# A Mamba-2 mixer with a 4-bit feed-forward layer: y and z laid out channel-major, the heads' products in two column tiles

## What is computed

```python
z, xBC, dt = split(u @ W_in)                 # z: 512 channels, x: 512, B: 128, C: 128, dt: 8
xBC = silu(causal_conv4(xBC) + conv_b)
x, B, C = split(xBC)
dt = softplus(dt + dt_bias);  A = -exp(A_log)
y = ssd(x * dt, A * dt, B, C)                # y_l = sum_{s<=l} (C_l.B_s) exp(sum_{s<r<=l} A dt_r) dt_s x_s
y = y + x * D                                # D: one number per head
y = y * silu(z)
y = y * rsqrt(mean(y**2) + eps) * norm_scale
x1 = layernorm(u + y @ W_out)
out = layernorm(x1 + ffn(x1))                # 256 -> 2048 -> 256, gate and up, 4-bit weights with scales
```

## Time and profile before

| | us |
|---|---|
| median of 3 runs | 983.26 (981.26 to 985.05) |
| profiled execution, its time | 982.58 |
| its span, first to last instruction | 980.8 |
| TensorE busy | 921.1 (94%) |
| VectorE busy | 682.8 (70%) |
| ScalarE busy | 535.3 (55%) |
| GpSimd busy | 85.0 (9%) |

### The profile page before, as it was taken

How to read it: one execution, slowest core, us unless ns; L and a number is a source line. 1 busy time by engine, 2 the same in 40 slices (tenths; PEclk the granted TensorE clock), 3 DMA queues, 4 the chain that set the end, 5 groups by cost and what they waited for, 6 DMA issues and landing times.

```text
span 980.8 us, 16203 instructions
## 1 busy us (share of the span) xinstructions
PE 921.1 (94%) x5452; PEld 798.0 (81%) x5452; DVE 682.8 (70%) x1390; ACT 535.3 (55%) x1056; POOL 85.0 (9%) x170
## 2 busy tenths in 40 slices
PE   4677889899999999999999999999999999999997
PEld 3446668788888888878888888878888889888887
DVE  6776667687758876687758766687759765776453
ACT  4643478357645576447645575447645674455232
POOL 2110000200002000200011000200011001100000
PEclk9797999899999999999999999999999999999999
DMA  4111000010001000020001000020001000000000
GB/s 132 31 57 48 25 23 22 1 55 1 20 3 66 0 0 21 0 65 0 22 0 65 0 0 21 1 65 0 22 0 65 1 2 12 22 33 1 1 33 11
DMA packets 18813, 23.28 MB, mean 24 GB/s; under 512 B 1728, under 2 KB 15296, under 8 KB 18752
## 3 DMA queue, kind: packets, MB, share of 16 engines
q1 hardware_dynamic: 18176, 22.56, 7.1%
q10 hardware_dynamic: 576, 0.03, 0.0%
HBM read 14.19 MB, written 4.19 MB: 19 GB/s over the span
## 4 chain that ended last, share of the span: by engine, by line
issue 54%; PE 31%; DVE 7%; POOL 4%; ACT 3%; DMA 1%; POOLq 0%; SPq 0%; DVEq 0%; ACTq 0%
PE up_bank L482 2%; PE mixer L562 2%; PE down L482 2%; PE down L483 2%; PE up_bank L484 2%; PE down L484 2%; PE up_bank L483 2%; PE gate_bank L482 2%; PE gate_bank L483 2%; PE gate_bank L484 2%; PE mixer L482 2%; PE mixer L484 2%; PE mixer L483 2%; DVE xbc L898 1%; PE down L642 1%
## 5 line engine op out<-in xcount | busy, mean ns | idle before, releaser
L482 PE MATMUL down<-wd_hi,in_hi 128*128 128x256 f32 x512 | 145.1, 283 | 0.6 <-DVE in_lo L1019 0.6
L483 PE MATMUL down<-wd_lo,in_hi 128*128 128x256 f32 x512 | 144.6, 282 | 0.0
L484 PE MATMUL down<-wd_hi,in_lo 128*128 128x256 f32 x512 | 144.3, 282 | 0.0
L898 DVE SCALAR_TENSOR_TENSOR xbc<-mixer,chan,xbc 128x510 f32<-128x510 f32 (+1 forms) x162 | 111.0, 685 | 32.9 <-ACT xbc L690 30.5
L768 ACT ACTIVATE act_sb<-gate_bank 128x512 f32<-128x512 f32 (+1 forms) x144 | 79.0, 549 | 86.1 <-PE gate_bank L484 84.9
L754 ACT ACTIVATE in_hi<-act_sb 128x512 fp32r<-128x512 f32 (+1 forms) x144 | 83.5, 580 | 68.9 <-PE down L484 55.5
L1033 DVE SCALAR_TENSOR_TENSOR act_sb<-up_bank,act_sb 128x512 f32<-128x512 f32 (+1 forms) x144 | 90.5, 628 | 40.1 <-PE up_bank L484 22.3
L482 PE MATMUL up_bank<-hT_hi,wu_hi 128*128 128x512 f32 (+1 forms) x288 | 108.2, 376 | 7.0 <-DVE act_sb L1033 6.8
L482 PE MATMUL gate_bank<-hT_hi,wg_hi 128*128 128x512 f32 (+1 forms) x288 | 114.2, 396 | 0.0
L484 PE MATMUL gate_bank<-hT_hi,wg_lo 128*128 128x512 f32 (+1 forms) x288 | 107.6, 374 | 0.0
L483 PE MATMUL gate_bank<-hT_lo,wg_hi 128*128 128x512 f32 (+1 forms) x288 | 107.1, 372 | 0.0
(11 more groups left out here) (201 smaller groups left out, 2031.7 us busy)
## 6 DMA issues: line engine op xcount, KB each, us to landing
xbc<-in_u_t_dram SPq DMA_DIRECT2D x7, 512.0 KB, 3.6
h_sb<-in_u_dram SPq DMA_DIRECT2D x7, 512.0 KB, 3.9
h_res<-h_sb SPq DMA_DIRECT2D x7, 512.0 KB, 2.9
out_dram<-h_res SPq DMA_DIRECT2D x7, 512.0 KB, 3.3
scales<-in_ffn_s_dram SPq DMA_DIRECT2D x24, 128.0 KB, 2.1
packed<-in_ffn_w_dram SPq DMA_DIRECT2D x8, 96.0 KB, 2.0
xbc<-in_u_t_dram SPq DMA_DIRECT2D x2, 256.0 KB, 2.8
xbc<-in_W_in_dram SPq DMA_DIRECT2D x1, 512.0 KB, 6.2
```

The lines of the kernel that those rows point to most:

```text
L482: nc.tensor.matmul(dst, lh, rh, start=first, stop=False, skip_group_check=True)
L483: nc.tensor.matmul(dst, lh, rl, start=False, stop=False, skip_group_check=True)
L484: return nc.tensor.matmul(dst, ll, rh, start=False, stop=last, skip_group_check=True)
L898: ins = stt(acc[:, :, d:], src[:, :, 0:SEQ - d], chan[:, c:c + 1], acc[:, :, d:], ALU.mult, ALU.add)
```

## The change

z is projected channel-major like x (4 blocks of 128 channels in every group, the halved groups too, which now have z2 and z3). In Y the operands change places: `xdt` (64 columns of a head) is stationary, the decay matrix of 128 columns is moved, and the even heads write partitions 0 to 63, the odd ones 64 to 127, each in a column tile of its own. y so comes out channel-major. D is now one number per partition, and x is used as it is, channel-major: VectorE's `x_d` adds it in four 128-column steps. The state's decay must now stand along the free axis, alike on all partitions of a head: a new product E, from the same R as D, in four 512-column matmuls per pair of tiles (two with 128 output rows, two with 64), and ScalarE's Exp of 512 columns of it in the item Y of odd tiles. The gated y needs no transpose: `gT` and its bank go. Its squares are added over blocks by VectorE and over partitions by a one-column matmul, S; VectorE scales that and GpSimd raises it to the power -1/2 in one step. CB loses its two 8-column matmuls. The load of the next transposed u waits for the last `x_d` instead of the last XT, since x is read longer. In the tables `gT` becomes `g`, and S is set into the slots:

```diff
 USES (full):
-             "D0a", "D0b", "Y0", "XT1", "D1a", "D1b", "Y1", "Yoff0", "CB1", "gT0", "XT2", "D2a", "D2b",
-             "op0", "gT1", "Y2", "XT3", "D3a", "D3b", "op1", "gT2", "Y3", "Yoff1", "op2", "gT3", "op3"],
+             "D0a", "D0b", "Y0", "XT1", "D1a", "D1b", "E0", "Y1", "Yoff0", "CB1", "XT2", "D2a", "D2b", "S0",
+             "op0", "Y2", "XT3", "D3a", "D3b", "E1", "S1", "op1", "Y3", "Yoff1", "S2", "op2", "S3", "op3"],
 SLOTS (full):
-             ["D0"], ["R1", "Y0", "XT1"], ["D1"], ["R2", "Y1", "CB1", "gT0", "XT2"], ["D2"],
-             ["R3", "op0", "gT1", "Y2", "XT3"], ["D3"], ["op1", "gT2", "Y3"], ["op2", "gT3"], ["op3", "ln1"], ["ln2"]],
+             ["D0"], ["R1", "Y0", "XT1"], ["D1"], ["R2", "Y1", "CB1", "g0", "XT2"], ["D2", "S0"],
+             ["R3", "op0", "g1", "Y2", "XT3"], ["D3", "S1"], ["op1", "g2", "Y3"], ["S2", "op2", "g3"],
+             ["S3", "op3", "ln1"], ["ln2"]],
...
+        D_ADDED, Y_DONE = (1, 4, 7, 10), (2, 6, 8, 12)
...
-                wait_for((ready(g - 1, f"XT{tiles(g - 1) - 1}")[0], g - 1, ready(g - 1, f"XT{tiles(g - 1) - 1}")[1]))
+                wait_for((y_step, g - 1, D_ADDED[tiles(g - 1) - 1]))
                 sp.dma_start(u32[:, :, 0:width(g)], uT_of(g)).then_inc(uT_in.sem, 16)
 TensorE:
-                    nc.tensor.matmul(b[:, 3 * P:3 * P + H], tri_r[:, :], dA_hi[:, 2 * i + 1, :],
-                                     start=True, stop=False)
-                    nc.tensor.matmul(b[:, 3 * P:3 * P + H], tri_r[:, :], dA_lo[:, 2 * i + 1, :],
-                                     start=False, stop=True).then_inc(ready(g, use)[0].sem, 1)
...
+                    if i % 2:
+                        use = f"E{i // 2}"
+                        wait_bank(pe, use, g)
+                        for a, rows in ((1, P), (0, HP)):
+                            for n, part in enumerate(R_of(g)):
+                                mm = nc.tensor.matmul(bank(g, use)[0:rows, :],
+                                                      tri_r[:, P - 1:P].to_broadcast([P, rows]), part[:, a::2, :],
+                                                      start=n == 0, stop=n == 1, skip_group_check=True)
...
                     for h in range(H):
-                        mm = nc.tensor.matmul(bank(g, use)[:, h * HP:(h + 1) * HP], dec_of(g, i)[:, h, :],
-                                              xdt[:, h * HP:(h + 1) * HP], start=True, stop=True)
+                        j, a = h // 2, h % 2
+                        mm = nc.tensor.matmul(bank(g, use)[a * HP:(a + 1) * HP, j * P:(j + 1) * P],
+                                              xdt[:, h * HP:(h + 1) * HP], dec_of(g, i)[:, h, :],
+                                              start=True, stop=True, tile_position=(0, a * HP), skip_group_check=True)
...
-                        nc.tensor.matmul(bank(g, use)[:, :], cb[:, 1, :], xtail[:, :], start=True,
-                                         stop=True).then_inc(ready(g, use)[0].sem, 1)
-                elif kind == "gT":
-                    use = f"gT{i}"
-                    wait_bank(pe, use, g)
-                    wait(pe, y_step, g, (3, 8, 11, 16)[i])
-                    for j in range(JT):
-                        mm = nc.tensor.transpose(bank(g, use)[:, j * P:(j + 1) * P],
-                                                 zs[:, i, j * P:(j + 1) * P], ident[:, :])
+                        for j in range(JT):
+                            mm = nc.tensor.matmul(bank(g, use)[:, j * P:(j + 1) * P], xtail[:, j * P:(j + 1) * P],
+                                                  cb[:, 1, :], start=True, stop=True)
+                elif kind == "S":
+                    wait_bank(pe, name, g)
+                    wait(pe, sq_sum, g, i + 1)
+                    nc.tensor.matmul(bank(g, name)[:, 0:1], y[:, i % 2, 0:P], tri[:, P - 1:P], start=True,
+                                     stop=True).then_inc(ready(g, name)[0].sem, 1)
 ScalarE:
-                        nc.scalar.activation(e2[:, i // 2, :], bank(g, f"CB{i // 2}")[:, 3 * P:3 * P + H],
-                                             ACT.Exp).then_inc(e2_ok.sem, 1)
...
+                elif kind == "Y":
+                    if i % 2:
+                        if i > 2:
+                            wait_ready(act, f"S{i - 2}", g)
+                        wait_ready(act, f"E{i // 2}", g)
+                        nc.scalar.activation(y[:, 1, :], bank(g, f"E{i // 2}")[:, :], ACT.Exp).then_inc(e_ok.sem, 1)
 VectorE:
-                    tt(head(y[:, i % 2, :]), head(bank(g, use)[:, :]),
-                       d_bc[:, :].unsqueeze(2).to_broadcast([P, H, HP]), ALU.mult).then_inc(y_step.sem, 1)
...
+                    if i % 2 == 0:
+                        wait_ready(dve, f"Y{i}", g)
+                        x_d(yc, bank(g, f"Y{i}"), i)
+                    else:
+                        wait_ready(dve, f"Yoff{i // 2}", g)
+                        wait(dve, e_ok, g, i // 2 + 1)
+                        tt(yc, bank(g, f"Yoff{i // 2}")[:, :], yc, ALU.mult).then_inc(y_step.sem, 1)
+                        x_d(yc, yc, i)
+                        tt(yc, bank(g, f"Y{i}")[:, :], yc, ALU.add).then_inc(y_step.sem, 1)
+                    tt(tile_of(zs, i), tile_of(zs, i), by_block(yc), ALU.mult).then_inc(y_step.sem, 1)
+                elif kind == "g":
+                    tt(q[:, 0:2 * P], q[:, 0:2 * P], q[:, 2 * P:4 * P], ALU.add).then_inc(sq_half.sem, 1)
+                    tt(q[:, 0:P], q[:, 0:P], q[:, P:2 * P], ALU.add).then_inc(sq_sum.sem, 1)
+                    tt(g_lo[:, :, :], tile_of(zs, i), f32(g_hi[:, :, :]), ALU.subtract).then_inc(g_l.sem, 1)
+            def x_d(dst, src, i):
+                for j in range(JT):
+                    at = (slice(None), slice(j * P, (j + 1) * P))
+                    ins = stt(dst[at], xbc[:, j, i * P:(i + 1) * P], chan[:, 34 + j:35 + j], src[at], ALU.mult, ALU.add)
```

More of the change, by code:

```diff
@@ L512, in mixer @@
                     mm.then_inc(ready(g, use)[0].sem, 1)
-                    if i == 4:
+                    if name == "x4":
                         dt_mm.then_inc(ready(g, "dt")[0].sem, 1)
-                elif kind == "z":
-                    use = f"z{i}"
-                    wait_bank(pe, use, g)
-                    for k in range(KT):
-                        mm = mm3(bank(g, use)[:, :], [x[:, k, i * P:(i + 1) * P] for x in (uT_hi, uT_lo)],
-                                 [w[:, k, 0:DI] for w in (win_hi, win_lo)], k == 0, k == KT - 1)
-                    mm.then_inc(ready(g, use)[0].sem, 1)
                 elif kind == "CB":
@@ L581, in mixer @@
                     wait_bank(pe, use, g)
-                    wait(pe, gT_l, g, i + 1)
+                    wait(pe, g_l, g, i + 1)
                     for j in range(JT):
-                        mm = mm3(bank(g, use)[:, 0:DM], [x[:, j * P:(j + 1) * P] for x in (gT_hi, gT_lo)],
+                        mm = mm3(bank(g, use)[:, 0:DM], [x[:, j, :] for x in (g_hi, g_lo)],
                                  [w[:, j, :] for w in (wout_hi, wout_lo)], j == 0, j == JT - 1)
@@ L669, in tanh @@
                 wait(act, conv, g, 3 * n + 3)
-                wait(act, ssq_ok, g - 1, tiles(g - 1))
+                wait_ready(act, f"S{tiles(g - 1) - 1}", g - 1)
                 if n >= 2:
@@ L687, in mixer @@
                     wait_ready(act, f"x{i}", g)
-                    wait_ready(act, f"XT{tiles(g - 1) - 1}", g - 1)
+                    wait(act, y_step, g - 1, D_ADDED[tiles(g - 1) - 1])
                     nc.scalar.activation(xbc[:, i, 0:width(g)], bank(g, f"x{i}")[:, 0:width(g)], ACT.Identity,
@@ L701, in mixer @@
                     wait_ready(act, f"z{i}", g)
[L702 to L705 removed]
+                    wait(act, g_l, g - 1, tiles(g - 1))
+                    nc.scalar.activation(zs[:, i, 0:width(g)], bank(g, f"z{i}")[:, 0:width(g)], ACT.Tanh, scale=0.5)\
                         .then_inc(z_tanh.sem, 1)
                 elif kind == "CB":
[L708 to L709 removed]
                     wait_ready(act, f"CB{i}", g)
@@ L953, in mixer @@
                 elif kind == "Y":
-                    s0 = (0, 3, 8, 11)[i]
-                    yc = y[:, i % 2, :]
-                    wait_ready(dve, f"Y{i}", g)
-                    wait(dve, y_step, g, s0 + 1)
-                    tt(yc, bank(g, f"Y{i}")[:, :], yc, ALU.add).then_inc(y_step.sem, 1)
-                    wait(dve, y_step, g, s0 + 2)
-                    s0 += 2
-                    if i % 2:
-                        use = f"Yoff{i // 2}"
-                        wait_ready(dve, use, g)
-                        wait(dve, e2_ok, g, i // 2 + 1)
-                        tt(head(xdt[:, :]), head(bank(g, use)[:, :]),
-                           e2[:, i // 2, :].unsqueeze(2).to_broadcast([P, H, HP]), ALU.mult)\
-                            .then_inc(y_step.sem, 1)
-                        wait(dve, y_step, g, s0 + 1)
-                        tt(yc, yc, xdt[:, :], ALU.add).then_inc(y_step.sem, 1)
```

(7 more changed lines are left out.)

149 lines of the change are left out of this document (72 added, 77 removed), and 16 rows, old and new, of tables (SLOTS, USES).

## The result

The changed kernel takes 989.06 us (median of 5 runs, 988.11 to 989.3) where the kernel before takes 984.61 on the same chip: the ratio is 1.0051, 95% interval 1.0036 to 1.0067. It is slower by half a per cent, which is little, but the interval leaves out 1. The forecast was 973 us. The profiled execution has 988.93 us, its span 987.2, against 980.8 before, so 6.4 us of span are to be explained, and 16.8 against the forecast's sum (980.8 less 10.4).

What follows compares the result with a forecast made beforehand. The prediction took TensorE's stream to bound full groups, and chains through VectorE and ScalarE the start. Groups 1 to 6 -12.8, LAST -1.1, group 0 +3.0, FIRST +0.5: minus 10.4, about 973 us, range 965 to 998.

Steps and rivals of the forecast that it cites:

- TensorE's stream, per full group: TensorE in full groups: products added and removed, overlapping Y and mode switches sum to minus 2.1 us per group.
- Rival 1: Y on TensorE: the column tiles don't overlap, plus 13.4 us in all, 996 us; chance 0.25.
- Rival 2: Y on TensorE: in a column tile loads no longer hide beside matmuls, plus 37, about 1020 us; chance 0.08.
- Rival 3: Slot 9 or 13: VectorE or ScalarE stalls TensorE about 1 us in each group, 979 us; chance 0.15.
- VectorE and ScalarE, per full group: Full groups: both stay below TensorE; the ninth slot, traced as having it all, keeps 0.5 to 1 us slack: zero.
- XT2 now waits for E0's bank: Ninth slot of full groups: the Exp reads that bank at 361.8, just when TensorE arrives; zero cost.
- Group 0: Half-length units at the start: Exp and table load delay Y's chains on VectorE; plus 3.0 us, bounds 0 and 5.
- The expected sign: End of group 0: TensorE's wait for h_sb longer by a microsecond and later by four.
- FIRST: First group: squares, x_d and adds lengthen op0's chain, overlapping Y takes some off; plus 0.5 us, bounds 0 and 2.5.
- LAST: Last group, two tiles: TensorE's savings as in full groups, minus 1.1 us.
- Columns streamed are the same: z on TensorE: swapped operands stream the same columns in full and half groups; zero cost.
- VectorE's plus 1.4 us per group and ScalarE's plus 6.3: Full groups: net extra VectorE work, and ScalarE's two Exps with table loads, both staying below TensorE.

Runs made afterwards that it cites:

- experiment 2: Changed kernel with ScalarE's Exp of E moved from Y's item to D's, behind the odd tiles' two Exps: 975.13 us, ratio 0.993 to the kernel before.
- experiment 3: experiment 1 with Y's heads issued 0, 2, 4, 6, then 1, 3, 5, 7: 994.21 us, ratio 1.0117 to the kernel before.
- experiment 8: experiment 2 plus the fourteen products of experiment 7 and LAST's z1 and z2 a slot forward: 969.58 us, ratio 0.9874 to the kernel before.
- experiment 9: Kernel before, with only fourteen products added ahead of the wait for h_sb at the end of group 0: 979.33 us, ratio 0.9963.
- experiment 1: Changed kernel with S1 ahead of E1 in the list of banks, issue order unchanged: 981.16 us, ratio 0.9987 to the kernel before.
- experiment 5: experiment 1 with a Copy in place of E's Exp, leaving out the decay's exponential and its table loads: 975.11 us, ratio 0.9904 to the kernel before.
- experiment 6: experiment 2 with one 512-column x_d operation in place of four, leaving out D's differences between blocks: 972.52 us, ratio 0.9877 to the kernel before.
- experiment 7: experiment 2 with fourteen overwritten products ahead of the wait for h_sb at the end of group 0: 970.86 us, ratio 0.9866 to the kernel before.
- experiment 10: Changed kernel, with only fourteen products added ahead of the wait for h_sb at the end of group 0: 984.34 us, ratio 1.0024 to the kernel before.

## Why the prediction was wrong

*TensorE's stream, per full group: right in sum.* Y 1.02 us per tile to the next start (forecast 0.97, and 1.82 with no overlap), E 0.92 twice (0.93), CB 0.15 less per pair (0.22 taken), Yoff 0.09 longer (zero taken), S 0.14 to the next start and 0.22 with what the product behind it is late (0.22 taken). Together a steady period 2.0 us shorter in experiment 2, where 2.1 was forecast. That agreement is in part luck: Yoff and CB came out dearer, gT was a little more to gain, and a switch costs more than was taken. The rule of the Trainium skill, "TensorEngine Tiling (Array Packing)", Key Properties, that different tiles can load and multiply in parallel, agrees with the paired starts told under experiment 3, of matmuls and of loads alike (0.007 us apart). Its other rule, that a switch drains the array, is named there without a price. In the trace Y's first record starts 0.21 us behind the product in front of it, where it was 0.115 before, and the product behind Y's last record starts 0.20 later, where it was 0.11. So a tile pays 0.19 us at its two edges, 0.09 of it inside the 1.02, where 0.10 was taken. That this is the drain is not shown.

*Rival 1, tiles that don't overlap:* excluded by experiment 3. *Rival 2, loads that no longer hide:* sixteen records in 1.02 us, 0.064 each, with a load of 0.136 us in the mean, leave no room for it. So the rule of the Trainium skill, "TensorE: Matmul & The Clock Gate", Part 3, The mechanism, that loads overlap matmuls only where the row group differs, doesn't describe this trace: the column tiles share theirs. The paragraph above it there also allows a load into a background weight buffer, and no run here tells the two apart.

*Rival 3, a stall of TensorE in slot 9 or 13 of each group: this is what came*, and it had 0.15. The forecast named "E's Exp" as a sign of it, but not the path, Yoff1 waiting for E1's bank, and the wait was 1.6 us rather than 1. Its 979 us were too low as well, as group 0 and LAST lost more than they had in the sum.

*The step that failed* is in "VectorE and ScalarE, per full group". The forecast followed the ninth slot alone, as the slot "that has it all", and asked of each engine whether it is late for VectorE's next unit. There it was right: no wait of TensorE for unit 9's product shows in groups 1 to 6. Of banks it looked at one, "XT2 now waits for E0's bank ... just when TensorE arrives", and put that at zero. The sister wait in slot 13 was never looked up: E1's reader stands a whole slot behind its writer, behind g2's copy, and four uses on is Yoff1. So a term that the sum put at zero is 1.6 us times six groups, 9.6 of the 12.8 forecast. up_bank's waits in slot 2 of four groups (3.45 us in all before, 4.30 after) and XT2's 0.8 in group 6 take 1.7 more, so that without these waits the six groups would have given 11.3; experiments 8 and 9 have 11.6 between them. The wait of XT2 was zero in steady groups, as said, but 1.4 us in group 0. A list of all uses in which the reader's place on its engine lies beyond the next use of its bank would have shown both.

*Group 0, forecast plus 3.0 with bounds 0 and 5: plus 5.3.* The mechanism was as told, the Exp with its load ahead of Y's chain on VectorE. Experiment 2 takes 4.7 of it back; by experiments 1 and 5, 0.9 of that is E1's bank, 1.9 the loads and 2.0 the place. What was left out: Yoff1's and XT2's bank waits (1.6 and 1.4 us), and longer waits of TensorE for ScalarE's part of the weights, 14.1 us in all in the rows of L654 above, and before:

```profile
PE down L642 <- ACT wg_lo L779: 5.5, 2, 4.9
PE down L642 <- ACT wd_lo L779: 3.1, 3, 1.8
PE down L642 <- ACT wu_lo L779: 2.0, 2, 1.1
```

10.6. They stay at 14.1 in experiment 8, where group 0 still costs 1.7 us. That these are the same microseconds was not tried. The expected sign, a wait for h_sb longer by a microsecond and later by four, was half right: the wait stayed at 3.56, and it ended 5.3 us later.

*FIRST, plus 0.5: measured 0.0.* It ends between 73.5 and 75.4 us in versions that differ little there, so the term was too small to judge.

*LAST, minus 1.1: measured plus 1.2*; without the fall of the clock described below it is minus 0.2, as in experiment 2. "Columns streamed are the same" was right of z's sum and wrong of its place: in LAST half of z's products went from slots 1 and 2, where they covered VectorE's convolution, to slots 3 and 4. TensorE comes 1.0 us earlier to unit 2 and waits 2.02 us instead of 1.21:

```profile
862.41 0.50 PE L482 MATMUL up_bank<-hT_hi,wu_hi 128*128 128x512 f32 x1 [1.21 <-DVE act_sb L1033]
```

In the changed kernel the clock then falls to 0.78 over 5 us. The profiles with this fall have 136.8 us or more for LAST and the end, the two with the same wait and no fall 135.5, so the fall is the other 1.4 us.

*VectorE's plus 1.4 us per group and ScalarE's plus 6.3*: VectorE has 15 us more in all (2.0 per full group, as x_d's steps are longer than taken), ScalarE 43 (thirty loads of 1.283 and the Exps). As totals they were hidden, as forecast. ScalarE's were harmful by place, never by sum.

## What to carry to other kernels

When an operation is added that uses a rotating buffer, write down for every use of the rotation where its reader stands in its own engine's queue, and what that reader waits for; a reader one slot behind its writer turns into a wait four uses later, of an instruction that needs nothing from it. Put an activation beside others of its table: with the same Exp ScalarE's busy time rose by 43 us in one place and by 3 in another. Products for different column tiles should alternate in program order, or most of the overlap is lost. And when two versions differ by less than a per cent, look at the granted clock behind each idle wait before giving the difference to the edit.

## What the runs showed of the hardware

The granted clock after an idle wait does not come back after a fixed time. The same wait of 3.55 us ahead of group 1 was followed by half clock to about 193 us in the kernel before (5 us) and to about 201 us in experiment 2 (13 us), with TensorE busy throughout; group 1 took 106.8 to 111.1 us in versions whose steady period was 107.7. So a difference of 4 us between two profiled executions can be the clock's alone, as between experiments 2 and 6. What decides how long it lasts is open. Fourteen useless products in that wait removed it in four kernels, and gave 0.4% where nothing else was changed (experiment 9).

Behind the wait of 2.0 us in LAST the clock fell to half for 3 to 4 us in six profiles (the changed kernel, experiments 1, 3, 5, 6 and 7), and did not in two with the same wait (experiments 2 and 10).

fp32 records of 128 columns followed each other every 0.109 us in one column tile, with weight loads of 0.136 us hidden. Two tiles ran at once, 0.007 us apart, when their products alternated; when they came grouped, the second tile started with three records of the first still to start.
